# Moving transposes, a transfer and three small steps in a two-layer kernel on one core

## The reference

```
x = x + linear_attention(ln(x))     # 16 heads of 8, running sums over time
x = x + experts(ln(x))              # 8 experts; each takes the 129 best tokens of each sequence
x = x + causal_attention(ln(x))     # 16 query heads, one key/value head of 8
x = x + filter(ln(x)) + bias        # real(ifft(fft(x) @ W)): one 128x128 matrix here
```

```
tokens = x[b, idx[b, e]]                        # gather
y = gelu(tokens @ w1[e] + b1[e]) @ w2[e] + b2[e]
out[b, idx[b, e]] += y * gate[b, e]             # scatter-add
```

## Time and profile before

| | us |
|---|---|
| three runs, median (lowest to highest) | 796.59 (795.17 to 796.68) |
| the profiled execution, by the same clock | 804.09 |
| its span, first to last instruction | 801.9 |
| PE busy, share of the span | 644.6, 80% |
| DVE busy | 548.5, 68% |
| POOL busy | 361.2, 45% |
| ACT busy | 353.9, 44% |

### The profile page before, as it was taken

How to read it: one execution, slowest core, us unless ns; L and a number is a source line. 1 busy time by engine, 2 the same in 40 slices (tenths; PEclk the granted TensorE clock), 3 DMA queues, 4 the chain that set the end, 5 groups by cost and what they waited for, 6 DMA issues and landing times.

```text
span 801.9 us, 14622 instructions
## 1 busy us (share of the span) xinstructions
PE 644.6 (80%) x4312; PEld 398.9 (50%) x4345; DVE 548.5 (68%) x1808; ACT 353.9 (44%) x764; POOL 361.2 (45%) x513
## 2 busy tenths in 40 slices
PE   1489898997206699999795569899999999999795
PEld 1246666664103478877584223454545454544453
DVE  8378888888691133243336797889898989898454
ACT  0323232320711222233231205776777777767883
POOL 0176555552007587788862102434434344333342
PEclk9999999999657799999997667999999999999998
DMA  9300000000231222223324440203131221300011
GB/s 297 106 1 1 0 1 0 0 1 1 78 106 49 32 43 41 41 42 43 44 25 102 52 59 4 60 16 50 26 41 31 34 41 25 50 15 2 17 54 40
DMA packets 42937, 33.51 MB, mean 42 GB/s; under 512 B 4144, under 2 KB 39520, under 8 KB 42864
## 3 DMA queue, kind: packets, MB, share of 16 engines
q1 hardware_dynamic: 32528, 24.62, 14.3%
q0 software_dynamic: 8992, 7.38, 6.4%
q10 hardware_dynamic: 1344, 0.62, 0.3%
HBM read 13.87 MB, written 8.91 MB: 28 GB/s over the span
## 4 chain that ended last, share of the span: by engine, by line
PE 45%; DVE 20%; POOL 13%; issue 12%; ACT 3%; DMA 2%; SPq 1%; DVEq 0%; ACTq 0%; POOLq 0%
PE bank L1982 8%; DVE masked L1574 7%; POOL x_dram L950 7%; POOL x_row L943 6%; PE wide L1969 5%; PE wide L639 4%; PE bank L1914 3%; PE bank L611 3%; PE wide L640 3%; PE bank L1121 2%; DVE st L292 2%; DVE mx L1574 2%; DVE prod L389 2%; PE wide L621 1%; PE bank L1994 1%
## 5 line engine op out<-in xcount | busy, mean ns | idle before, releaser
L1761 ACT ACTIVATE pexp<-wide 128x512 f32<-128x512 f32 (+2 forms) x384 | 181.3, 535 | 73.4 <-PE wide L1969 70.2
L1685 POOL TENSOR_SCALAR_AFFINE_SELECT pexp<-pexp 128x256 f32<-128x256 f32 x256 | 106.1, 418 | 185.7 <-ACT pexp L1761 183.7
L1574 DVE CUSTOM_DVE_ANT_0 masked<-bank,mask_qk 128x384 f32<-128x384 f32 (+3 forms) x356 | 154.0, 481 | 18.6 <-PE bank L1914 17.7
L1969 PE MATMUL wide<-qT,kTe 128*128 128x256 bf16 (+3 forms) x501 | 119.7, 301 | 6.6 <-ACT pexp L1761 2.5
L1092 ACT ACTIVATE hT<-wide,b1T 128x512 f32<-128x512 f32 x64 | 43.8, 687 | 147.1 <-PE wide L1112 112.8
L1914 PE MATMUL bank<-kTm,qT 128*128 128x384 bf16 (+3 forms) x348 | 87.1, 318 | 18.9 <-DVE mx L1574 9.4
L950 POOL DMA_INDIRECT x_dram<-yg,row_u x48 | 76.2, 1588 | 31.5 <-DVE yg L999 18.6
L1574 DVE CUSTOM_DVE_ANT_0 masked<-wide,mask_qk 128x256 f32<-128x256 f32 (+3 forms) x156 | 74.2, 498 | 17.8 <-PE wide L1914 17.8
L943 POOL DMA_INDIRECT x_row<-xln_dram,row_u x64 | 62.4, 975 | 52.8 <-DVE slot_tok L819 33.6
L1982 PE MATMUL bank<-pexp,vx 128*32 128x512 f32 (+3 forms) x1024 | 83.9, 439 | 0.5 <-POOL pexp L1685 0.5
L1121 PE MATMUL bank<-w_sb,hT 128*128 128x128 f32 x512 | 71.6, 283 | 5.0 <-issue 5.0
(11 more groups left out here) (273 smaller groups left out, 1056.0 us busy)
## 6 DMA issues: line engine op xcount, KB each, us to landing
qT<-qp SPq DMA_DIRECT2D x144, 64.0 KB
x_sb<-in_L_attn_x SPq DMA_DIRECT2D x8, 256.0 KB, 6.7
w_sb<-in_L_ffn_w SPq DMA_DIRECT2D x1, 2048.0 KB, 13.3
xln_dram<-rx SPq DMA_DIRECT2D x8, 256.0 KB, 2.3
out_x<-x_sb SPq DMA_DIRECT2D x7, 256.0 KB, 2.3
x_dram<-x_sb SPq DMA_DIRECT2D x6, 256.0 KB, 3.6
x_sb<-x_dram SPq DMA_DIRECT2D x6, 256.0 KB, 2.8
x_row<-xln_dram,row_u POOLq DMA_INDIRECT x64
```

Of the source, the lines that this page charges most:

```text
L1574: ins = nc.vector.tensor_tensor_reduce(out=masked[:, n % 4, at], in0=bank_of(n)[:, at], in1=mask_qk[:, T - w:T], scale=1.0, scalar=LEAST, ...
L1685: nc.gpsimd.affine_select(out=pexp[:, at, :, 0:P], in_=pexp[:, at, :, 0:P], pattern=[[0, 2], [1, P]], compare_op=ALU.is_ge, fill=0.0, base ...
L1761: nc.scalar.activation(pexp[:, exp_slot(b, 2 * step + h // 2), h % 2:h % 2 + nh, 0:w], scores_bank(b, m)[:, 0:nh * w].rearrange("p (h t) - ...
L1969: ins = nc.tensor.matmul(scores_bank(b, m)[:, hh * w:(hh + 1) * w], kTe[:, par, j * P:(j + 1) * P], qT[:, b % QB, 4 * qd + h + hh, j * P:T ...
```

## The change

Four things are changed.
1. The experts on PE: the transposes of the second half's first gather come before all hidden pieces, and those of phase p+2 stand at step i = 2 of phase p and no more at i = 0. They stand ahead of the side work of that step.
2. In the passage, ACT issues the nine row DMAs of the first sequence's half 1, three at a time between its copies; SP had issued them after half 0's.
3. In the passage, DVE takes the first `rstd` before it adds sequence 7; q's other parts come before the fifth statistics; PE issues four scores ahead of the second sequence's k and v; ACT loads the table for exp after the second normalisation.
4. At the end, the residual of `SEQ[6]` is added by POOL, from a copy that ACT makes of the product; DVE adds the bias of the last sequence.

DVE's list within the experts is the same as before.

```diff
         def moe_pe(pe):
             pe.wait_ge(s_we.sem, s_we.total(16 * NWE))
             pe_moe_xT(pe, 0, 0)
+            pe.wait_ge(r_slotT.sem, r_slotT.total(3))
+            pe_moe_xT(pe, 0, 1)
             for c in range(HC):
                 pe_moe_hidden(pe, 0, c)
-            pe.wait_ge(r_slotT.sem, r_slotT.total(3))
-            pe_moe_xT(pe, 0, 1)
...
-                    if i == 0 and p + 2 < PHASES:
+                    if i == 2 and p + 2 < PHASES:
                         pe_moe_xT(pe, e + 1, half)
                     pe_moe_side(pe, e, half, i)
                     pe_moe_output(pe, p, i)
...
+        def dve_end_bias(dve, half):
+            part = x_sb[:, SEQ[B - 1], end_tiles(half), :]
+            nc.vector.tensor_tensor(part, part, fb_sb[:, :].unsqueeze(1).broadcast_to([P, END_TILES, D]), ALU.add).then_inc(f_b.sem, 1)
...
+        product_sb = masked[:, 0, :]
+
+        def act_end_product(act):
+            act.wait_ge(f_yp.sem, f_yp.at(B - 2, 1))
+            nc.scalar.activation(product_sb, psFY[:, :], ACT.Copy).then_inc(f_pc.sem, 1)
+
+        def pool_end_filter(pool):
+            x6 = x_sb[:, SEQ[B - 2]]
             pool.wait_ge(f_xln.sem, f_xln.at(B - 2, 1))
...
+            pool.wait_ge(f_pc.sem, f_pc.total(1))
+            nc.gpsimd.tensor_tensor(x6, x6, product_sb.rearrange("p (k d) -> p k d", d=D), ALU.add).then_inc(f_x.sem, 1)
...
             dve_var_eps(dve, ln3, 0, 1)
-            dve_moe_add(dve, last_scatter(SEQ[1]), SEQ[1])
             dve_inverse(dve, 0, 1, 3)
             dve_ln3_shift(dve, 0, 1)
+            dve_moe_add(dve, last_scatter(SEQ[1]), SEQ[1])
             dve_moe_stats(dve, 1)
-            for n in range(2, 5):
+            for n in range(2, 4):
                 dve_moe_add_rest(dve, SEQ[n])
                 dve_moe_stats(dve, n)
+            dve_moe_add_rest(dve, SEQ[4])
             dve_q_parts(dve, 0, range(1, SPLITS))
+            dve_moe_stats(dve, 4)
...
             for half in range(2):
                 dve_end_xln(dve, half)
-            dve_filter_residual(dve, B - 2)
+            dve.wait_ge(f_b.sem, f_b.at(B - 2, 1))
+            for half in range(2):
+                dve_end_bias(dve, half)
...
             act_q_first_part(act, 0)
+            act.wait_ge(s_zero.sem, s_zero.total(2))
+            q_rows(act, 0, 1, (0,))
             act_kv(act, 0)
-            act.wait_ge(s_zero.sem, s_zero.total(2))
+            q_rows(act, 0, 1, (1,))
             act_first_kT(act, 0)
+            q_rows(act, 0, 1, (2,))
             act_std(act, 1, B, 4, preset=False)
-            act_preset(act, ACT.Exp)
             act.wait_ge(s_shift.sem, s_shift.total(4))
             act_xln(act, 1)
+            act_preset(act, ACT.Exp)
...
             act_filter_xT(act, B - 2)
+            act_end_product(act)
...
             q_rows(sp, 0, 0)
-            q_rows(sp, 0, 1)
             q_rows(sp, 1, 0)
...
+            pe_max_at_start(pe, range(2 * PER_QUAD, 2 * PER_QUAD + len(psM4)))
             pe_kv(pe, 1)
-            pe_max_at_start(pe, range(2 * PER_QUAD, 3 * PER_QUAD))
+            pe_max_at_start(pe, range(2 * PER_QUAD + len(psM4), 3 * PER_QUAD))
```

More of the change, by code:

```diff
@@ L1224, in build @@
         F = lambda name, per=1, step=1: signal("filter_" + name, per, step)
+        f_pc = F("product_copied")
         f_c, f_xln, f_xTp, f_xT, f_yp, f_b, f_x, f_out = (
@@ L1435, in dve_end_filter_residual @@
             dve.wait_ge(f_b.sem, f_b.at(B - 1, half + 1))
+            if half == 0:
+                dve.wait_ge(f_x.sem, f_x.at(B - 2, 1))
             nc.vector.tensor_tensor(part, part, by_tile(psE_product[half])[:, end_tiles(half), :], ALU.add).then_inc(f_x.sem, 1)
@@ L1503, in act_end_xln @@
             ins.then_inc(f_xln.sem, 1)
-        def pool_end_bias(pool):
-            bias = lambda n: fb_sb[:, :].unsqueeze(1).broadcast_to([P, n, D])
-            pool.wait_ge(f_xln.sem, f_xln.at(B - 2, 1))
[L1508 to L1512, removed]
+        product_sb = masked[:, 0, :]
[4 more added lines that the diff above has]
+            x6 = x_sb[:, SEQ[B - 2]]
+            pool.wait_ge(f_xln.sem, f_xln.at(B - 2, 1))
+            nc.gpsimd.tensor_tensor(x6, x6, fb_sb[:, :].unsqueeze(1).broadcast_to([P, NT, D]), ALU.add).then_inc(f_b.sem, 1)
+            pool.wait_ge(f_b.sem, f_b.at(B - 2, 1))
+            pool.wait_ge(f_pc.sem, f_pc.total(1))
+            nc.gpsimd.tensor_tensor(x6, x6, product_sb.rearrange("p (k d) -> p k d", d=D), ALU.add).then_inc(f_x.sem, 1)
         def fill_k_slots(ops, n):
@@ L1710, in mqa_pool @@
                 pool_turn(pool, b, middle=b + 1 < B, front=b + 2 < B)
-            pool_end_bias(pool)
+            pool_end_filter(pool)
         def act_xln(act, b, tiles=range(NT)):
@@ L1840, in mqa_act, with q_rows @@
                 act_end_xT(act, half)
-        def q_rows(queue, b, half):
+        def q_rows(queue, b, half, parts=range(PARTS)):
             if b >= QB:
                 queue.wait_ge(q_sp.sem, q_sp.at(b - QB, NS))
-            for n in range(PARTS):
+            for n in parts:
                 queue.wait_ge(q_qpart.sem, q_qpart.at(b, min(2 * n + 1, SPLITS)))
```

## The result

| | us |
|---|---|
| before, median of 4 (lowest to highest) | 796.44 (795.17 to 796.68) |
| after, median of 4 (lowest to highest) | 805.27 (805.13 to 811.47) |
| ratio, 95% interval | 1.0133 (1.0084 to 1.0182) |
| forecast (range) | 806.3 (799.5 to 812.5) |
| profiled execution of after; its span | 805.25; 803.3 |

What follows compares the result with a forecast made beforehand. PE was taken to bound the experts until about 375 us, POOL's gathers until the last landing, then PE again. Experts +7.6, passage +0.7, +2.5 and -0.8, end -0.3: +9.7 on 796.59 gives 806.3 us (799.5 to 812.5).

Steps and rivals of the forecast that it cites:

- The waits for `side`: Experts: PE waits for DVE's add behind its copy, six times 1.67 us and once 2.67, together +12.7.
- The gathers' waits: Experts: later transposes cover PE's three late waits for gathers, the last of 3.21 us: -4.9.
- None of my terms rests on it: Claim that no forecast term depends on the place where ACT idles 12.81 us and POOL's first scatter waits 5.53.
- PE sets the pace until about 375 us.: Experts: PE, 30.00 of 30 us busy, sets the pace until then; POOL's gathers do until the last landing.
- POOL stays the bound: Rival, 7%: experts' waits for `side` fall into time PE would spend waiting for the last gather; faster, 793.5 us.
- The clock (-1.7): Experts, near 400 us: without the 3.21 us wait TensorE does not fall to its lower clock, -1.7 us.
- the start (+1.5): Start of the experts: hidden pieces begin only after the second transposes; first output piece later, +1.5 us (0 to 2.5).
- The rows on two queues: Passage: half 1's row DMAs on ACT run beside half 0's and delay the first scores, +2.5 us (0 to 8.7).
- The rival of full sharing: Passage, rival, 15%: both queues share the DMA engines; 8 us instead of 2.5, total 811.8.
- k and v, the root: Passage: four scores ahead of k and v, -0.8 (0 to -1.2); DVE waiting for the first root, +0.7.
- The end: Last sequences' residuals and biases: POOL no longer adds beside DVE's 0.76 us step, -0.3 us (-0.6 to +0.5).
- Its rival (800 us): Rival, 6%: the early standstill is real without a profiler and the new order is past it, -5.5 to -7.

Runs made afterwards that it cites:

- the trace shown: Kernel before with the end part alone (POOL adds the seventh residual from ACT's copy, DVE the last biases): 795.41 us against 796.16, ratio 0.999.
- the mean of five: Traces of the five experiments on the kernel before that left the experts alone and had no standstill: experts 171.5 to 172.5 us in four, 172.9 in the fifth.
- undisturbed executions: Executions of the kernel before without ACT's 12.81 us standstill; experts taken as 172.2 us, against 179.47 in before's own profile.

## Why the prediction was right, and where it was wrong

- **The waits for `side`.** Right in mechanism and number (six and one). Mis-sized: 1.47 instead of 1.67 each, since DVE picks up 0.03 us behind the transposes, not 0.20, and starts the add 0.61 behind the copy's start; and 2.17 instead of 2.67, since the two 0/1 matrices also hold the add up by 0.7 and not by 1.0. 11.0, not 12.7.
- **The gathers' waits.** The step that failed in the experts: "-4.9" is -8.3 in the trace shown and -7.8 in the mean of five. It was read from a profile whose experts had stood still near 265 us. During that time POOL went on gathering, so the waits later were 3 us smaller than in the undisturbed executions. "None of my terms rests on it" was wrong.
- **"PE sets the pace until about 375 us."** PE's 30.00 of 30 and POOL's 22.12 did not tell them apart: POOL's busy time leaves out the 0.3 us ahead of each of its 19 instructions, 5.7 of the 30, and with them it was at 27.8 of 30. In undisturbed executions it had nothing to spare. The rival "POOL stays the bound" had this half of the mechanism. It didn't decide, for with the waits for `side` PE came to the last gathers late enough: after has no wait for them, and there it is POOL that waits for DVE's gate, 2.16 and 2.33 us at 325 and 336.
- **The clock (-1.7) and the start (+1.5).** The clock is right: 23.3 us from the last transposes to the last gate, where undisturbed before has 28.5, is the -3.5 of order and -1.7 of clock. The start was sized a little low: the fifth transposes come 31.1 us behind the first in after, 27.6 without the 3.5 of order, and 25.2 to 26.0 undisturbed, so +2.1 within the bounds 0 to 2.5. The measured terms, 11.0 - 7.8 - 1.7 + 2.1 = 3.6, give the 3.4 of the table.
- **The rows on two queues.** The largest error: +7.7 and not +2.5, though in the bounds 0 to 8.7. The step that failed is the choice near none because the two DMAs' destinations are often different partitions. That doesn't matter here: the eight engines that are busy are the ones that every such DMA uses. The rival of full sharing, which I gave 15%, was right. The first scores did wait for q's rows, until 457.6 on the old time scale (449.3 + 0.6 + 7.7) and not until my 452.5. The rate that was to tell the case (68 or 130) told it: 66.
- **k and v, the root.** +0.6 as forecast (+0.7); -1.3 instead of -0.8, just beyond its bound of -1.2.
- **The end.** DVE's last chain comes 0.6 later and not sooner: POOL's add falls beside DVE's shortest instruction. The 2.0 us of tail were in no term: the prediction has nothing on what follows the last output, POOL's closing instruction above all. They turn the part to a gain of 1.4 in the traces. The 0.3 for the step that POOL had slowed came as forecast (0.42 instead of 0.76 us).
- **The standstill.** Its rival (800 us) had 6%. It did not decide: before's profile has 7.3 us more in the experts than the undisturbed ones and is 7.7 us over the median, so the timed runs of before went without it, and so did after's profile, at 805.25 beside its median of 805.27. Where it comes up it costs about 10 to 15 us on the spot, of which before gets some back, because the late gathers have then landed. One of the four runs of after, 811.47, lies 6.2 us above the others; whether that was a standstill isn't known. What causes it stays open.

Experts -4.2, queue +5.2, the rest -1.9: the errors cancel to -0.9. The total came out right by luck, by the sum of these errors and not by the working.

## What to carry to other kernels

Before a stage is called one engine's, add to each engine's busy time what stands between its instructions: an engine in DMA issues can be full at 80% busy, and then work saved elsewhere comes back as its wait. A transfer is put on a second queue only if it uses other DMA engines; count the packets that end its shares. An add that frees a buffer belongs ahead of whatever else in its engine's list waits for the same partner. And POOL's last work belongs early: its closing instruction took 6.2 us in every trace here, so it sets the end of the program unless POOL is done more than 4.2 us ahead of the last instruction whose result is written out (6.18 + 0.23 - 2.27).

## What the hardware showed that I had not expected

- A DMA of 64 KB into 8 partitions has eight shares, and all such DMAs of SP's and ACT's queue together move 66 to 68 GB/s; a like one into 64 partitions has sixteen, and beside it the sum was 89.
- POOL's closing DRAIN ends 6.18 to 6.26 us behind its last add in all fourteen traces; with POOL's add 2.1 us ahead of DVE's last instruction it sets the end of the program, 2.2 us behind the last output's landing.
- A DVE instruction of 0.17 us took 1.11 or 1.12 beside a POOL add with two inputs in SBUF, and ended with it, in all six traces with the new end.
- ACT can stand for 9 to 15 us at the same place of a program in some executions with its input there; no transfer, clock or wait in the records goes with it.
